# Masked queries in two halves, a product split around a score row, and row statistics one maximum later

## The chip, the cores and the metric

The kernel runs on one core of a Trainium2 chip. The metric is the device time of one execution in microseconds. A core has four compute engines that run their own in-order instruction streams and meet only at semaphores: TensorE (PE in the profile, its weight loads PEld), VectorE (DVE), ScalarE (ACT) and GpSimd (POOL). SyncE (SP) starts the transfers.

## The reference

32 sequences of 100 query rows and 361 context rows, width 256, pass through four layers. Each layer adds its result to x:

```python
x = x + xattn0(layernorm(x), ctx)       # 16 heads of 16, softmax(q k^T / 4) v
x = x + ffn0(layernorm(x))              # one of 8 experts per token, by argmax
x = x + xattn1(layernorm(x), ctx)       # 8 heads of 32, own layernorms and output product
x = x + ffn1(layernorm(x))              # two of 8 gated experts per token

# the part that the change touches, xattn0, for one sequence:
Q = layernorm(x) @ Wq + bq;  K, V = split(ctx @ Wkv + bkv)
scores = einsum('qhd,khd->hqk', Q, K) / 4      # 16 heads
out = einsum('hqk,khd->qhd', softmax(scores), V)
```

## The kernel before

The function `attention` is built twice, for layer 0 (the first attention) and layer 1. It takes one sequence, called a batch, at a time, and it is pipelined by hand: the step of batch b ("a round") does the front of batch b+1, the body of batch b, the tail of batch b-1, and prepares the context and rows of batch b+2. The names are `nxt` = b+1, `nxt2` = b+2, `prev` = b-1. Every engine has its own `step` (for VectorE `step0` in layer 0), and the order in which it calls things is the order of execution. Rounds run from t = -1 to 32. A tail is there from t = 1 on, and a batch t+2 to prepare until t = 29, so that both are there in the 29 rounds from 1 to 29. Rounds 4 to 27 are a loop on each engine, the others are written out.

What a round of layer 0 contains, as far as the change touches it:

- **Queries.** TensorE projects them into PSUM bank M0. ScalarE writes them with their bias to `qf` (L680), one instruction for each of the two 128-channel halves, and signals `qf_ready` after the second. VectorE multiplies `qf` by a mask, so that a group of 32 partitions holds one head of 16 at a time, into `QM` (L999, `masked_queries`), 128 partitions by 400 elements in one instruction.
- **Exact maxima.** Softmax needs each row's maximum. TensorE computes the scores of two heads at a time into the two banks of SM (`score_rows`, L453, rows 0 to 7), VectorE reduces them (`maxima`, L1008). SM holds only one pair, so row j waits for maximum j-1 (`max_done`), and maximum j waits for row j. Rows 0 and 1 read the first half of `QM`, row 2 the first of those that read the second.
- **Values.** The value product has three tiles of keys. `project_rest` (tile 2) and `project_first` (tile 0, into M0, so after `qf` has been read) are six matmuls each (L383), and both stand between row 0 and row 1 on TensorE. Then come `scores(b, 1)` (L478, L485), row 2, and so on.
- **Finished rows.** The rows of `prev` need their mean and variance: VectorE's `residual_stats(prev)` (L970, L977, L978) signals `var_ready`. GpSimd's `power(1, prev)` waits for it and runs four small instructions (L780, L786, L788, L792).
- **GpSimd's order.** `masked_max(b)`, `attended(prev)` (L808, adds the attention's output to the rows), `power(1, prev)`, `low_parts(nxt)` (L843, L848), `power(0, nxt2)`, `low_context(nxt2)` (L854, writes `cl`, the low part of the context), `attended_twice`, `masked_low`, `value_bias`. It is strictly in this order.
- **Keys of the batch after next.** After row 6, TensorE's `start_k` calls `first_k(nxt2)`, whose first instruction waits for `cl_ready`, which is what L854 signals. Behind it stand row 7, the transposes of `avs`, and the `front` of the next round.

```python
def first_k(b):
    pe.wait_ge(cl_ready, b.count(1, 1))
    project_k(b, 0)
```

Of the kernel before, what the change touches and what calls it, by code (L numbers as in the profile page):

```python
# [19 lines left out]
ALU = mybir.AluOpType  # L20
ACT = mybir.ActivationFunctionType
# [107 lines left out]
def attention(nc, layer, t, env):  # L129
# [7 lines left out]
    NG = H // HG  # L137
    NP = H // 2
    NS = 3
    AHEAD = 5 + layer  # L140
    SCALE = 0.25 if layer == 0 else 1.0 / 16.0
    LAG = 2 * layer
# [16 lines left out]
    with ExitStack() as ctx:  # L159
# [216 lines left out]

        @block.tensor
        def _(pe):
            def summed(out, pairs):

                steps = [(c, lhs, rhs) for c in range(DC) for lhs, rhs in pairs]
                for k, (c, lhs, rhs) in enumerate(steps):
                    last = nc.tensor.matmul(out, lhs(c), rhs(c), start=(k == 0), stop=(k == len(steps) - 1))  # L383
                return last

# [7 lines left out]

                summed(M1[:, 0:LKP], [(w(wkh), x(ch)), (w(wkh), x(cl)), (w(wkl), x(ch))]).then_inc(k_ps, 1)

            def project_v(b, kt, M, c0):
                k0, n = KTILES[kt]

                def x(context):
                    return lambda c: context[b.p][:, c, k0:k0 + n]  # L400

                def w(weights):
                    return lambda c: weights[:, c, :]

                return summed(M[0:n, c0:c0 + D], [(x(ch), w(wvh)), (x(ch), w(wvl)), (x(cl), w(wvh))])

            def first_k(b):
                pe.wait_ge(cl_ready, b.count(1, 1))
# [25 lines left out]
            def project_rest(b):  # L434
                project_v(b, 2, M1, D).then_inc(v_ps, 1)

            def project_first(b):
                pe.wait_ge(qf_ready, b.count(1, 1))
                last = project_v(b, 0, M0, 0)
                if layer == 1:  # L440
                    for c in range(DC):
                        last = nc.tensor.transpose(M0[0:LQ, D + c * 128:D + (c + 1) * 128], qf[:, c, :], ident[:])
                last.then_inc(v_ps, 1)

            def score_rows(b, j):

                if j == 0:
                    pe.wait_ge(kt_ready, b.count(1, 1))
                    pe.wait_ge(qm_ready, b.count(1, 1))
                pe.wait_ge(max_done, b.count(NP, j))  # L450
                for half in range(2):
                    rows, chunk, m = place(half * NP + j)
                    last = nc.tensor.matmul(SM[0:LQ, half, 0:LKP], QM[b.p][rows, chunk, m, :], KT[b.p][rows, chunk, :],  # L453
                                            start=True, stop=True)
                last.then_inc(sm_ps, 1)
# [88 lines left out]
            def step(b, fr, ahead, back, tail):  # L544
                nxt, nxt2, prev = b.plus(1), b.plus(2), b.plus(-1)

                def rows_of(*pairs):
                    if fr:
                        for j in pairs:
                            score_rows(nxt, j)  # L550

                if fr:
                    front(nxt)
                if back:
                    max_columns(b)
                if fr:
                    project(nxt)
                if back:
                    scores(b, 0)
                rows_of(*((0,), ())[layer])  # L560
                if fr:
                    project_rest(nxt)
                    project_first(nxt)
                rows_of(*((1,), (0,))[layer])
                if back:
                    scores(b, 1)
                rows_of(*((2,), (1,))[layer])
                if back:
                    free_m0(nxt, fr)
                    values(b, 0)  # L570
                rows_of(*((3,), ())[layer])
                if back:
                    scores(b, 2)
                rows_of(*((4,), (2,))[layer])
                if tail:
                    if fr:
                        pe.wait_ge(v_evac, nxt.count(2, 1))
                    out_transposes(prev, layer == 1, prev.low >= LAG)
                if back:
                    values(b, 1)  # L580
                rows_of(*((5,), ())[layer])
                if tail:
                    out_product(prev, layer == 1, prev.low >= LAG)
                if back:
                    values(b, 2).then_inc(av_ps, 1)
                rows_of(*((6,), (3,))[layer])
                if ahead:
                    start_k(nxt, nxt2, prev, tail)
                rows_of(*((7,), ())[layer])
                if back:  # L590
                    pe.wait_ge(avs_copied, b.count(1, 1))
                    for g in range(NG):
                        last = nc.tensor.transpose(ST[0:LQ, 0, g * 128:(g + 1) * 128], avs[:, g, :], ident[:])
                    last.then_inc(avt_ps, 1)
# [15 lines left out]
        def _(act):  # L610
# [7 lines left out]
            def split_k(b):  # L618

                act.wait_ge(k_evac, b.count(2, 2))  # L620
                if b.low >= 2:
                    act.wait_ge(st_ps, b.count(NS, -NS))
                nc.scalar.activation(KT[b.p][:], KF[:], ACT.Copy).then_inc(kt_ready, 1)  # L623
                act.wait_ge(qf_ready, b.count(1, 1))
                if layer == 0:
                    nc.scalar.activation(q_hi[:], qf[:], ACT.Copy).then_inc(q_hi_ready, 1)
                else:
                    nc.scalar.activation(QM[b.p][:, :, 0, :], qf[:], ACT.Copy).then_inc(qm_ready, 1)
# [45 lines left out]

            def projected(b):
                act.wait_ge(q_ps, b.count(1, 1))
                act.wait_ge(qm_ready, b.count(1))
                act.wait_ge(ql_ready, b.count(1))
                for h in range(DC):
                    last = nc.scalar.activation(qf[:, h, :], M0[:, h * LQ:(h + 1) * LQ], ACT.Identity,  # L680
                                                bias=bq[:, h:h + 1])
                last.then_inc(qf_ready, 1)
                split_k(b)

            def values_out(b):
# [83 lines left out]
        def _(pool):  # L769
# [68 lines left out]
            def low_parts(b):  # L838

                pool.wait_ge(kt_ready, b.count(1, 1))  # L840
                if b.low >= 2:
                    pool.wait_ge(st_ps, b.count(NS, -NS))
                nc.gpsimd.tensor_tensor(KL[b.p][:], KF[:], KT[b.p][:], ALU.subtract).then_inc(kl_ready, 1)  # L843
                if layer == 0:
                    pool.wait_ge(q_hi_ready, b.count(1, 1))
                    pool.wait_ge(qm_ready, b.count(1, 1))
                    pool.wait_ge(ql_ready, b.count(1))
                    nc.gpsimd.tensor_tensor(qf[:], qf[:], q_hi[:], ALU.subtract).then_inc(q_lo_ready, 1)  # L848

# [6 lines left out]
            def masked_low(b):  # L856

                if b.low >= 1:
                    pool.wait_ge(st_ps, b.count(NS))
                if layer == 1:  # L860
                    pool.wait_ge(qm_ready, b.count(1, 1))
                    nc.gpsimd.tensor_tensor(QL[:, :, 0, :], qf[:], QM[b.p][:, :, 0, :], ALU.subtract
                                            ).then_inc(ql_ready, 1)
                    return
                pool.wait_ge(q_lo_ready, b.count(1, 1))
                nc.gpsimd.tensor_tensor(
                    QL[:], qf[:].unsqueeze(2).to_broadcast([128, DC, HT, LQ]),
                    mask[:].unsqueeze(1).unsqueeze(3).to_broadcast([128, DC, HT, LQ]), ALU.mult).then_inc(ql_ready, 1)
# [86 lines left out]
        def _(dve):  # L955
# [37 lines left out]
                norm_stats(0, b, xrow(b))  # L993

            def masked_queries(b):
                dve.wait_ge(qf_ready, b.count(1, 1))
                if b.low >= 2:
                    dve.wait_ge(st_ps, b.count(NS, -NS))
                V_.tensor_tensor(  # L999
                    QM[b.p][:], qf[:].unsqueeze(2).to_broadcast([128, DC, HT, LQ]),  # L1000
                    mask[:].unsqueeze(1).unsqueeze(3).to_broadcast([128, DC, HT, LQ]), ALU.mult).then_inc(qm_ready, 1)

            def maxima(b, j):
                if j == 0:
# [84 lines left out]
            def step0(b, fr, ahead, back, tail):  # L1089
# [3 lines left out]
                for j in range(NP):  # L1093
                    if tail and j == 6:
                        take_product(prev, False, True)
                    if fr:
                        maxima(nxt, j)
                    if tail and j == 0:
                        residual(prev)
                        residual_stats(prev)  # L1100
                    if ahead and j == 1:
                        if nxt2.low == 1:
                            dve.wait_ge(x_more_loaded, 16)
                        moments(xrow(nxt2))
                    if ahead and j == 2:
                        variance(0, nxt2)
                if fr:
                    repeat_max(nxt)
# [1044 lines left out]
```

## Time and profile before

| | us |
|---|---|
| median of three runs | 1679.92 |
| lowest and highest | 1678.1, 1680.39 |
| the profiled execution | 1681.28 |
| its span, first to last instruction | 1679.5 |
| of it first attention | up to about 530 |
| second attention | about 820 to 1330 |

The profiled execution is 1.36 us above the median, and 1.78 us of its time lie outside its span. Busy time of an engine is a share of the whole span and says nothing of one stage. In a timeline the idle time in brackets is that of the engine just before the instruction, and the arrow names what it waited for; "issue" means that nothing in the profile shows a cause.

### The profile page before, as it was taken

Reading aid. Unit: us, or ns where it says so; the run is one execution under the profiler, and the core shown is the slowest. Engines: PE = TensorE matmul, PEld = TensorE weight load, DVE = VectorE, ACT = ScalarE, POOL = GpSimd, SP = SyncE. Lnnn points to the kernel's source line nnn. Section 1 sums busy time; section 2 is a strip of 40 time slices with the busy share of each in tenths; the row PEclk is TensorE's granted clock in tenths of the full one; section 3 lists DMA queues with packets and bytes.
Section 4 is the critical chain, followed back from the end, with each engine's and each line's share of the span. In section 5 each row is a group of like instructions: output and inputs, shape, how many; then the busy total and the mean of one; then the engine's idle time right before and its main releaser. Section 6 shows DMA issues by size and latency. Waiting matters only on the chain. (4 is left out here: it accounts for less than half of the span.)

```text
span 1679.5 us, 50228 instructions
## 1 busy us (share of the span) xinstructions
PE 1479.6 (88%) x17142; PEld 1237.9 (74%) x17143; DVE 985.4 (59%) x2196; ACT 880.9 (52%) x1626; POOL 838.1 (50%) x1145
## 2 busy tenths in 40 slices
PE   6999999999998299999689999999999925999958
PEld 4777777777776199999668888888888713888746
DVE  3666666666664323333236777777777558777745
ACT  3677777777775144444156566656665422333333
POOL 3566766656664111111146666666766414333275
PEclk7999999999998599999889999999999855999979
DMA  5121121111000611111212222222111041333377
GB/s 145 35 73 59 53 78 59 48 34 34 23 26 9 257 32 37 37 34 35 72 46 61 78 73 90 73 66 73 40 48 34 18 144 49 130 129 129 117 233 236
DMA packets 63184, 127.98 MB, mean 76 GB/s; under 512 B 11106, under 2 KB 35870, under 8 KB 59590
## 3 DMA queue, kind: packets, MB, share of 16 engines
q1 hardware_dynamic: 52798, 99.03, 18.1%
q0 software_dynamic: 10320, 28.07, 6.0%
q8 instruction: 41, 0.67, 0.2%
q14 instruction: 25, 0.20, 0.0%
HBM read 94.77 MB, written 32.29 MB: 76 GB/s over the span
## 5 line engine op out<-in xcount | busy, mean ns | idle before, releaser
L1008 DVE TENSOR_REDUCE a_mx<-a_SM 100x2 bf16<-100x722 f32 x384 | 351.4, 915 | 219.9 <-PE a_SM L453 215.2
L730 ACT ACTIVATE a_Pr<-a_ST 120x1600 f32<-120x1600 f32 (+3 forms) x192 | 225.0, 1172 | 134.6 <-PE a_ST L485 132.7
L780 POOL TENSOR_TENSOR a_rstd<-a_ve,a_powers 100x1 f32<-100x1 f32 x192 | 119.1, 620 | 161.5 <-DVE a_ve L978 161.3
L453 PE MATMUL a_SM<-a_KT,a_QM 32*100 32x362 f32 x768 | 155.4, 401 | 44.6 <-DVE a_mx L1008 40.0
L495 PE MATMUL a_M<-a_Pr,a_V 120*32 120x100 f32 (+3 forms) x4608 | 176.9, 257 | 0.0
L495 PEld LDWEIGHTS a_M<-a_Pr,a_V 120*32 120x32 f32 (+3 forms) x4608 | 136.3, 121 | 21.4 <-issue 12.7
L453 PEld LDWEIGHTS a_SM<-a_KT,a_QM 32*100 32x100 f32 x768 | 62.6, 159 | 102.2 <-DVE a_mx L1008 75.9
L854 POOL TENSOR_TENSOR a_cl<-a_ct,a_ch 128x724 fp32r<-128x724 f32 x62 | 107.2, 1728 | 43.1 <-DVE a_o L1050 43.1
L1531 PEld LDWEIGHTS e_PH<-e_xT,e_wS 128*128 128x128 f32 x1024 | 120.7, 194 | 4.4 <-issue 2.8
L1531 PE MATMUL e_PH<-e_xT,e_wS 128*128 128x128 f32 x1024 | 121.2, 277 | 2.3 <-DVE e_xT L1610 2.3
L383 PE MATMUL a_M<-a_wvh,a_ch 128*120 128x256 f32 (+1 forms) x384 | 120.9, 315 | 2.6 <-ACT a_KF L615 2.6
L1544 PE MATMUL e_PY<-w,e_hT 128*128 x512 | 117.7, 384 | 2.6 <-issue 2.6
L843 POOL TENSOR_TENSOR a_KL<-a_KF,a_KT 128x724 fp32r<-128x724 f32 x64 | 111.0, 1734 | 16.0 <-ACT a_KT L623 16.0
L383 PE MATMUL a_M<-a_ch,a_wkh 128*128 128x362 f32 x256 | 99.3, 388 | 18.3 <-POOL a_cl L935 18.1
L383 PE MATMUL a_M<-a_wvl,a_ch 128*120 128x256 f32 (+1 forms) x384 | 108.8, 283 | 0.0
L383 PE MATMUL a_M<-a_wvh,a_cl 128*120 128x256 f32 (+1 forms) x384 | 108.6, 283 | 0.0
L1544 PEld LDWEIGHTS e_PY<-w,e_hT 128*128 128x128 f32 x512 | 96.0, 192 | 15.3 <-issue 3.2
L485 PE MATMUL a_ST<-a_QM,a_KT 32*120 32x100 f32 (+3 forms) x1536 | 103.5, 305 | 0.0
L1575 ACT ACTIVATE e_hT<-e_PH,e_b 128x128 f32<-128x128 f32 x128 | 36.5, 368 | 124.4 <-PE e_PH L1531 124.4
L1497 POOL COPY e_gidx<-toks 128x1 int32 (+1 forms) x32 | 5.8, 181 | 189.8 <-PE e_PX L1518 166.2
L615 ACT ACTIVATE a_KF<-a_M,a_bk 128x362 f32<-128x362 f32 x128 | 71.7, 560 | 47.8 <-PE a_M L383 47.6
L1818 PE MATMUL g_PH<-w_high,g_xTh 128*128 x228 | 96.3, 422 | 0.0
(219 smaller groups left out, 3860.6 us busy)
## 6 DMA issues: line engine op xcount, KB each, us to landing
w<-in_E_w SPq DMA_DIRECT2D x24, 1024.0 KB, 6.9
a_ct<-in_ctx SPq DMA_DIRECT2D x64, 362.0 KB, 3.0
gated_rows<-g_hs SPq DMA_DIRECT2D x57, 256.0 KB, 2.4
keep_rows<-a_keep SPq DMA_DIRECT2D x64, 100.0 KB
tile_rows<-e_y SPq DMA_DIRECT2D x32, 128.0 KB
X<-in_E_b SPq DMA_DIRECT2D x1, 4096.0 KB, 17.6
x_rows<-X SPq DMA_DIRECT2D x32, 100.0 KB
g_xr<-x_rows SPq DMA_DIRECT2D x25, 128.0 KB, 3.8
```

The lines of the kernel that those rows point to most:

```text
L383: last = nc.tensor.matmul(out, lhs(c), rhs(c), start=(k == 0), stop=(k == len(steps) - 1))
L453: last = nc.tensor.matmul(SM[0:LQ, half, 0:LKP], QM[b.p][rows, chunk, m, :], KT[b.p][rows, chunk, :], start=True, stop=True)
L485: last = nc.tensor.matmul(ST[0:n, r, t * LQ:(t + HT) * LQ], K[rows, chunk, k0:k0 + n], Q[rows, chunk, :, :], start=False, stop=(k == 2 and ...
L495: last = nc.tensor.matmul(M0[VW * j:VW * (j + 1), g * LQ:(g + 1) * LQ], V[b.p][0:n, kt, h, :], Pr[0:n, kt, POS[h] * LQ:(POS[h] + 1) * LQ], ...
L730: nc.scalar.activation(Pr[0:n, s, :].rearrange("p (r q) -> p r q", r=GROUPS), ST[0:n, :, 0:PER * LQ], ACT.Exp, scale=SCALE).then_inc(exp_d ...
L780: nc.gpsimd.tensor_tensor(rstd[k][:], ve[k][:].to_broadcast([LQ, n]), powers[:, 0:n], ALU.pow).then_inc(rstd_ready[k], 1)
L843: nc.gpsimd.tensor_tensor(KL[b.p][:], KF[:], KT[b.p][:], ALU.subtract).then_inc(kl_ready, 1)
L854: nc.gpsimd.tensor_tensor(cl[b.p][:], ct[b.p][:], ch[b.p][:], ALU.subtract).then_inc(cl_ready, 1)
L1008: V_.tensor_reduce(pair, SM[0:LQ, :, 0:LK], AX_X, ALU.max).then_inc(max_done, 1)
L1531: last = nc.tensor.matmul(PH[:, p, g // 4, g % 4, :], lhs, xT[:, c, :], start=(c == 0), stop=(c == DC - 1))
L1544: last = nc.tensor.matmul(PY[:, p, 0:D], hT[p][:, g, :], rhs, start=(g == 0), stop=(g == G - 1))
L1818: last = nc.tensor.matmul(PH[:, p, h, :], x[p][:, c, :], rhs, start=(k == 0), stop=(k == len(steps) - 1))
```

## The change

The masked queries are made in two instructions, one for each half of the channels, and each can start when ScalarE has written its half of `qf`. Row 0 waits for the first half only, and row 2 has a wait of its own for the second. The value product of the first tile of keys is cut in two: three matmuls before row 1 and three behind it. The statistics of the finished rows move from behind maximum 0 to behind maximum 1, and those of the batch after next by one maximum as well (moments behind maximum 2, variance behind maximum 3). In layer 1 only the count of `qf_ready` changes. All of the diff but its context lines, with the places where only a count changed cut to one each:

```diff
+    QS = 2 - layer
...
-            def summed(out, pairs):
+            def summed(out, pairs, part=None):
                 steps = [(c, lhs, rhs) for c in range(DC) for lhs, rhs in pairs]
                 for k, (c, lhs, rhs) in enumerate(steps):
+                    if part is not None and c != part:
+                        continue
...
-            def project_first(b):
-                pe.wait_ge(qf_ready, b.count(1, 1))
-                last = project_v(b, 0, M0, 0)
+            def project_first(b, part=None):
+                pe.wait_ge(qf_ready, b.count(DC, DC))
+                last = project_v(b, 0, M0, 0, part)
...
-                last.then_inc(v_ps, 1)
+                if part != 0:
+                    last.then_inc(v_ps, 1)
             def score_rows(b, j):
                 if j == 0:
                     pe.wait_ge(kt_ready, b.count(1, 1))
-                    pe.wait_ge(qm_ready, b.count(1, 1))
+                    pe.wait_ge(qm_ready, b.count(QS, 1))
+                if layer == 0 and j == HT:
+                    pe.wait_ge(qm_ready, b.count(QS, 2))
...
                 if fr:
                     project_rest(nxt)
-                    project_first(nxt)
+                    project_first(nxt, (0, None)[layer])
                 rows_of(*((1,), (0,))[layer])
+                if fr and layer == 0:
+                    project_first(nxt, 1)
                 if back:
                     scores(b, 1)
...
                 for h in range(DC):
-                    last = nc.scalar.activation(qf[:, h, :], M0[:, h * LQ:(h + 1) * LQ], ACT.Identity,
-                                                bias=bq[:, h:h + 1])
-                last.then_inc(qf_ready, 1)
+                    nc.scalar.activation(qf[:, h, :], M0[:, h * LQ:(h + 1) * LQ], ACT.Identity,
+                                         bias=bq[:, h:h + 1]).then_inc(qf_ready, 1)
...
             def masked_queries(b):
-                dve.wait_ge(qf_ready, b.count(1, 1))
                 if b.low >= 2:
                     dve.wait_ge(st_ps, b.count(NS, -NS))
-                V_.tensor_tensor(
-                    QM[b.p][:], qf[:].unsqueeze(2).to_broadcast([128, DC, HT, LQ]),
-                    mask[:].unsqueeze(1).unsqueeze(3).to_broadcast([128, DC, HT, LQ]), ALU.mult).then_inc(qm_ready, 1)
+                for h in range(DC):
+                    dve.wait_ge(qf_ready, b.count(DC, h + 1))
+                    V_.tensor_tensor(
+                        QM[b.p][:, h], qf[:, h, :].unsqueeze(1).to_broadcast([128, HT, LQ]),
+                        mask[:].unsqueeze(2).to_broadcast([128, HT, LQ]), ALU.mult).then_inc(qm_ready, 1)
...
-                    if tail and j == 0:
+                    if tail and j == 1:
                         residual(prev)
                         residual_stats(prev)
-                    if ahead and j == 1:
+                    if ahead and j == 2:
                         if nxt2.low == 1:
                             dve.wait_ge(x_more_loaded, 16)
                         moments(xrow(nxt2))
-                    if ahead and j == 2:
+                    if ahead and j == 3:
                         variance(0, nxt2)
```

## Rows read from the trace of the kernel before

**Rows 1.** The profile's page, part 1, busy time by engine.

```profile
PE 1479.6 (88%) x17142; PEld 1237.9 (74%) x17143; DVE 985.4 (59%) x2196; ACT 880.9 (52%) x1626; POOL 838.1 (50%) x1145
```

**Rows 2.** Windows: stretch, length, then busy us (instructions) by engine, clock, DMA, GB/s.

```profile
32.00:48.00 16.00, 12.61 (x191) 10.34 (x194) 6.04 (x10) 8.94 (x14) 5.97 (x7) 0.70 0.04 11
48.00:64.00 16.00, 15.06 (x260) 12.19 (x257) 10.64 (x20) 11.42 (x20) 8.55 (x13) 1.00 0.08 27
66.50:512.00 445.50, 420.03 (x6946) 339.87 (x6944) 290.51 (x560) 319.60 (x561) 292.34 (x393) 1.00 0.16 48
```

**Rows 3.** Waits of 0 to 560 us: us in total, times, longest us.

```profile
POOL a_rstd L780 <- DVE a_ve L978: 85.6, 34, 5.8
PE a_SM L453 <- DVE a_QM L999: 3.9, 12, 0.4
```

**Rows 4.** Timeline, VectorE, 214.8 to 218.3: start, duration, instruction [idle before it <- releaser].

```profile
214.85 0.92 DVE L1008 TENSOR_REDUCE a_mx<-a_SM 100x2 bf16<-100x722 f32 x1 [0.74 <-PE a_SM L453]
...
216.49 0.15 DVE L978 TENSOR_SCALAR a_ve<-a_mv 100x1 f32<-100x1 f32 x1
216.80 0.92 DVE L1008 TENSOR_REDUCE a_mx<-a_SM 100x2 bf16<-100x722 f32 x1 [0.16 <-PE a_SM L453]
...
218.22 0.92 DVE L1008 TENSOR_REDUCE a_mx<-a_SM 100x2 bf16<-100x722 f32 x1 [0.17 <-PE a_SM L453]
```

**Rows 5.** Timeline, GpSimd, 216.7 to 223.7 us.

```profile
216.73 0.71 POOL L780 TENSOR_TENSOR a_rstd<-a_ve,a_powers 100x2 f32<-100x2 f32 x1 [3.04 <-DVE a_ve L978]
...
217.99 0.26 POOL L788 TENSOR_SCALAR a_nmr<-a_mv,a_rstd 100x1 f32<-100x1 f32 x1
...
220.98 0.55 POOL L780 TENSOR_TENSOR a_rstd<-a_ve,a_powers 100x1 f32<-100x1 f32 x1
...
221.96 1.73 POOL L854 TENSOR_TENSOR a_cl<-a_ct,a_ch 128x724 fp32r<-128x724 f32 x1
```

**Rows 6.** Timeline, TensorE and its weight loads, 215.7 to 225.3 us.

```profile
215.79 0.28 PE L383 MATMUL a_M<-a_wvh,a_cl 128*121 128x256 f32 x1
...
216.15 0.28 PE L383 MATMUL a_M<-a_wvh,a_cl 128*121 128x256 f32 x1
...
216.35 0.41 PE L453 MATMUL a_SM<-a_KT,a_QM 32*100 32x362 f32 x2
...
217.78 0.40 PE L453 MATMUL a_SM<-a_KT,a_QM 32*100 32x362 f32 x2 [0.23 <-DVE a_mx L1008]
...
224.04 0.19 PEld L383 LDWEIGHTS a_M<-a_ch,a_wkh 128*128 128x128 f32 x1 [0.17 <-issue]
...
225.23 0.16 PEld L453 LDWEIGHTS a_SM<-a_KT,a_QM 32*100 32x100 f32 x2 [0.23 <-DVE a_mx L1008]
```

**Rows 7.** Timeline, the first round with finished rows, and the last of the 29.

```profile
63.26 1.73 POOL L854 TENSOR_TENSOR a_cl<-a_ct,a_ch 128x724 fp32r<-128x724 f32 x1
...
65.11 0.19 PEld L383 LDWEIGHTS a_M<-a_ch,a_wkh 128*128 128x128 f32 x1 [0.37 <-issue]
...
510.58 0.19 PEld L383 LDWEIGHTS a_M<-a_ch,a_wkh 128*128 128x128 f32 x1 [0.17 <-issue]
```

**Rows 8.** Timeline, two rounds that follow each other, around the masked queries.

```profile
212.95 0.73 POOL L808 TENSOR_TENSOR X<-X,a_o 100x256 f32 x1
213.03 1.08 DVE L999 TENSOR_TENSOR a_QM<-a_qf,a_mask 128x400 fp32r<-128x400 f32 x1 [1.59 <-ACT a_qf L680]
...
214.41 0.41 PE L453 MATMUL a_SM<-a_KT,a_QM 32*100 32x362 f32 x2 [0.35 <-DVE a_QM L999]
...
229.19 0.58 DVE L999 TENSOR_TENSOR a_QM<-a_qf,a_mask 128x400 fp32r<-128x400 f32 x1 [1.57 <-ACT a_qf L680]
...
230.59 0.92 DVE L1008 TENSOR_REDUCE a_mx<-a_SM 100x2 bf16<-100x722 f32 x1 [0.82 <-PE a_SM L453]
```

**Rows 9.** Timeline, ScalarE, 219.0 to 220.5 us.

```profile
219.01 0.59 ACT L646 ACTIVATE a_xp<-X,a_nmr,a_rstd 100x256 f32 x1
220.45 1.51 ACT L730 ACTIVATE a_Pr<-a_ST 120x1600 f32<-120x1600 f32 x1 [0.85 <-PE a_ST L485]
```

More of the change, by code:

```diff
@@ L394, in project_k, with project_v @@
                 summed(M1[:, 0:LKP], [(w(wkh), x(ch)), (w(wkh), x(cl)), (w(wkl), x(ch))]).then_inc(k_ps, 1)
-            def project_v(b, kt, M, c0):
+            def project_v(b, kt, M, c0, part=None):
                 k0, n = KTILES[kt]
@@ L403, in w @@
                     return lambda c: weights[:, c, :]
-                return summed(M[0:n, c0:c0 + D], [(x(ch), w(wvh)), (x(ch), w(wvl)), (x(cl), w(wvh))])
+                return summed(M[0:n, c0:c0 + D], [(x(ch), w(wvh)), (x(ch), w(wvl)), (x(cl), w(wvh))], part)
             def first_k(b):
@@ L623, in split_k @@
                 nc.scalar.activation(KT[b.p][:], KF[:], ACT.Copy).then_inc(kt_ready, 1)
-                act.wait_ge(qf_ready, b.count(1, 1))
+                act.wait_ge(qf_ready, b.count(DC, DC))
                 if layer == 0:
@@ L676, in projected @@
                 act.wait_ge(q_ps, b.count(1, 1))
-                act.wait_ge(qm_ready, b.count(1))
+                act.wait_ge(qm_ready, b.count(QS))
                 act.wait_ge(ql_ready, b.count(1))
                 for h in range(DC):
-                    last = nc.scalar.activation(qf[:, h, :], M0[:, h * LQ:(h + 1) * LQ], ACT.Identity,
-                                                bias=bq[:, h:h + 1])
-                last.then_inc(qf_ready, 1)
+                    nc.scalar.activation(qf[:, h, :], M0[:, h * LQ:(h + 1) * LQ], ACT.Identity,
+                                         bias=bq[:, h:h + 1]).then_inc(qf_ready, 1)
                 split_k(b)
@@ L845, in low_parts @@
                     pool.wait_ge(q_hi_ready, b.count(1, 1))
-                    pool.wait_ge(qm_ready, b.count(1, 1))
+                    pool.wait_ge(qm_ready, b.count(QS, QS))
                     pool.wait_ge(ql_ready, b.count(1))
@@ L860, in masked_low @@
                 if layer == 1:
-                    pool.wait_ge(qm_ready, b.count(1, 1))
+                    pool.wait_ge(qm_ready, b.count(QS, QS))
                     nc.gpsimd.tensor_tensor(QL[:, :, 0, :], qf[:], QM[b.p][:, :, 0, :], ALU.subtract
```

## The prediction

> **What bounds the kernel now.** I read the page's busy times first: TensorE works 88% of the span, every other engine under 60% [rows 1]. The windows say how full it is where the change is made: 420.0 of 445.5 us, 94%, at the full clock (2.4 GHz), in the stretch that holds 28 rounds [rows 2]. So there is about 0.9 us of TensorE idle time per round to win, and the change only reorders; it takes no matmul away. The waits come next. GpSimd is idle for 85.6 us in front of its first power instruction, waiting for VectorE's variance of the finished rows [rows 3], the very thing that the change makes later. The timeline of one round then shows what each late start would touch. I count from maximum 0 of a round, here 214.85 [rows 4].
>
> - The variance (L978) starts at 216.49, 1.64 after maximum 0; GpSimd's power starts 0.24 later, having been idle for 3.04 us [rows 4, 5].
> - From there GpSimd has no slack: the four small instructions, L843, L848, the next power, its product and L854 follow each other, and `cl` is finished at 221.96 + 1.73 = 223.69 [rows 5]. That is 7.20 us behind the variance's start and 8.84 behind maximum 0.
> - TensorE loads the first weights of `first_k`, which waits for `cl`, at 224.04 [rows 6], 0.35 behind its end. What a real wait leaves between them is seen in round 1, where GpSimd was a little later: `cl` ended at 63.26 + 1.73 = 64.99 and the load came at 65.11, 0.12 later [rows 7]. So the usable slack of this chain is 0.35 - 0.12 = 0.23 us. It is this number that decides.
>
> The 3.04 us for which GpSimd is idle look like room, but they lie ahead of the chain, and the chain's start is what moves.
>
> **The change part by part.**
>
> *Statistics one maximum on.* They cost the same, but begin behind maximum 1 instead of behind maximum 0. The split product lets row 1 start sooner: it starts at 216.35 now, 0.20 behind the start of the twelfth matmul of the two products (216.15), though maximum 0 ended at 214.85 + 0.92 = 215.77. The ninth started at 215.79 [rows 4, 6]. With three matmuls moved behind it, row 1 can start 0.20 behind the ninth, at 215.99, and maximum 1 is 0.36 sooner than now, 1.95 - 0.36 = 1.59 behind maximum 0. The bounds are 1.42, the distance of maxima whose row waits only for its maximum (216.80 and 218.22) [rows 4, 6], and 1.95, no move at all. I take 1.59. So the variance starts 1.59 later, at 3.23 behind maximum 0. `cl` is ready at 3.23 + 7.20 = 10.43, and `first_k` starts at 10.55, against 9.19 now: TensorE stands still for about 1.35 us in front of it. Queued behind `first_k` are row 7, hence maximum 7, the repeated maxima, the avs transposes and the whole front of the next round. None of it can slip ahead.
>
> *What happens from `first_k` to the next maximum 0.* In the round that ends at 230.59 this took 230.59 - 224.04 = 6.55 us, with no wait for the masked queries; the other kind of round waits 0.35 us for them in front of row 0, and there are 12 such waits, 3.9 us in all [rows 3, 6, 8]. Row 7's weight load, which now has 0.23 us of waiting for maximum 6 in front of it [rows 6], finds that maximum long done. TensorE itself had no gap there, so I take 0.05 of it. 6.50 for every round. New period: 10.55 + 6.50 = 17.05 us.
>
> *Masked queries in halves.* The instruction takes 0.58 us when it starts ahead of GpSimd's L808, and 1.08 when L808 has started 0.08 before it [rows 8]. The first half can start when the first half of `qf` is there, earlier by one ScalarE instruction, so ahead of L808 in either round, and it does not have to wait. By the rows this is worth 0.4 us in every other round. The bounds are nothing (the half still collides) and 3.9 us over the stage, plus what the odd rounds are longer by. VectorE issues one instruction more; the nearest row gives it between 0.29 (half of 0.58) and 0.58 us, into idle time of 1.6 us in front and 0.7 behind [rows 4, 8]. I take no cost for it.
>
> The Trainium skill (SBUF — State Buffer, "SBUF: two separate sides") says that VectorE and GpSimd share a pair of ports by an exclusive lock, and the one that starts first holds it for its whole instruction. The two durations above agree. By that rule the first half escapes the wait and the second may be caught behind L808, up to 0.7 us, which row 2, three microseconds on, doesn't notice. Without it half of the rounds would keep their 0.4 us: 14 x 0.4 = 5.6 us more in the sum.
>
> *The split product.* The same six matmuls. What row 1 gains on its way (0.36 us) is spent before `first_k` and lost in the wait there. Only rounds outside the 29 keep it: the two at the start and round 30. 3 x 0.36 = 1.1 us of gain. The extra waits (for `qf` behind row 1, for the second half at row 2) are satisfied when reached. The nearest row of a satisfied wait shows 0.17 us on the weight queue alone [rows 6]; two of them lie before the stall. Nothing to 0.3 us, taken as nothing.
>
> *The other engines.* ScalarE's L646 for the finished rows needs GpSimd's product and lies at 219.01 now, behind the second exponential [rows 9]. That product was ready at 217.99 + 0.26 = 218.25 [rows 5]; 1.59 later is 219.84, and L646 takes 0.59, to about 220.5. The third exponential starts at 220.45 [rows 9], so it is pushed by less than 0.1. If it were pushed by 0.5, the values that follow it on TensorE would still be done before `first_k` may start, since all of that lies ahead of the stall; so it costs nothing, and the same holds for the input rows on ScalarE. VectorE's second statistics come one maximum later too, ahead of GpSimd's late second power (220.98 + 1.59 = 222.57) [rows 5]. No step that moved issues a transfer. SyncE's load of a context behind `cl_ready` is issued 1.35 us later and is used two rounds on.
>
> *Sum.* Round 1 is late by the full 1.59, since it already waited [rows 7]. The 28 periods between its `first_k` and that of round 29 took 510.58 - 65.11 = 445.47 us [rows 7], 15.91 each (the loop's two kinds of round, and shorter ones outside it). They become 28 x 17.05 = 477.4. Change: 477.4 - 445.5 + 1.6 - 1.1 = +32.4 us. On the profiled execution, 1681.28 with its span of 1679.5, that is 1713.7; it was 1.36 above the median, so 1712.3 for the median. The second attention only counts a semaphore differently and costs nothing.
>
> **The rivals.**
>
> 1. *The cover holds, and it is faster.* It needs the chain from variance to `cl` to have 1.59 us of slack. Then 12 rounds lose their 0.4 us wait (4.5 us) and all 29 about 0.2 us, the wait of row 2 for maximum 1 [rows 6]: -10, 1670. For it: GpSimd's 3.04 us of idle time. Against it: 0.35 between `cl` and its reader. It turns to slower as soon as the chain is late by more than about 0.23 + 0.4 us.
> 2. *The stall is paid and given back.* If the waits behind `first_k` (0.74 us of VectorE before maximum 0 [rows 4], 0.35 of TensorE) were not behind it in order but beside it, half of the stall would be absorbed: 29 x 0.6 = +17, 1697. Against it: everything there descends from `first_k` or stands behind it in a queue.
> 3. *Row 1 does not move up.* If it still starts 1.5 us behind maximum 0, the statistics are late by 1.95 instead of 1.59: 29 x 0.36 more, +10, 1723. Against it: row 1 follows the last product at 0.20 [rows 6], so fewer products must bring it forward.
> 4. *The clock falls.* TensorE would be busy 15.0 of 17.05 us, 88%. It ran at full clock at 94% (15.06 of 16) and partly at half (1.2 GHz) in the window with 79%, where it completed 191 matmuls against 260 [rows 2]. At that pace a round takes 17.05 x 260 / 191 = 23.2: 29 x 6.2 = 180 more, about 1892. The Trainium skill (TensorE: Matmul & The Clock Gate, "What's actually happening") makes the half rate the default and activity what lifts it. By that rule the stall would have to count as inactivity.
> 5. *Nothing measurable.* The chain is late by just what the faster rows give back. 1680.
>
> **How the numbers follow.** The forecast has 82%, the rivals in their order 4, 5, 4, 2 and 3%. The forecast's own bounds: down by 0.17 us per round if row 1 waits only for maximum 0 (1.42) and by 0.1 if row 7's whole wait is saved, 28 x 0.27 = 7.6, to 1704.7; up by 5.6 if the halves still collide, to 1717.9. With a microsecond of scatter I give 1703.5 to 1719. A change under 0.2% (3.4 us) is about what this kernel's measurement cannot tell from none. Faster 4%, same 3%, slower 93%.
>
> **What would show it.** In the profile after: the lines of waits have TensorE or its weight queue idle for about 1.3 us in front of L383 for GpSimd's `cl`, 29 times. Maximum 1 starts 1.59 behind maximum 0, the variance 3.23, `cl` ends at 10.43, and rounds are 17.05 us long without two kinds. The first masked half is not stretched. Layer 1 and the expert stages keep their times. I am wrong if `first_k` is not released by GpSimd, if the row after the split waits for something else, or if ScalarE's late L646 holds the third exponential back by more than some tenths (that would come on top).

## The result

The changed kernel takes 1725.84 us (median of four runs, 1721.02 to 1729.78) against 1680.03 for the kernel before: a ratio of 1.027, 95% interval 1.0255 to 1.0287. It is slower by 45.8 us; forecast were 32.4 us and a range that ends at 1719. The profiled execution took 1729.78, with a span of 1728.0.

The page after, part 1, answers to [rows 1]: the same number of matmuls, with TensorE busy 23 us longer, since part of them ran slower.

```profile
PE 1502.2 (87%) x17142; PEld 1248.7 (72%) x17143; DVE 1000.5 (58%) x2228; ACT 883.4 (51%) x1626; POOL 835.7 (48%) x1145
```

The waits of 0 to 610 us after the change answer to [rows 3]. TensorE's wait for `cl` is new, 29 times; GpSimd's wait for the variance is longer; no row waits for the masked queries any more.

```profile
POOL a_rstd L787 <- DVE a_ve L985: 133.9, 34, 8.4
...
PE a_M L386 <- POOL a_cl L861: 37.7, 29, 1.8
```

The timeline after the change: the first weight load of `first_k` in round 1, a round that nothing disturbs, whose maximum 0 is at 165.00, and `first_k` in round 29. The lines of `attention` lie a little lower now: L808 is L815, L843 is L850, L854 is L861, L978 is L985, L999 is L1007, L1008 is L1016.

```profile
67.84 0.19 PEld L386 LDWEIGHTS a_M<-a_ch,a_wkh 128*128 128x128 f32 x1 [1.99 <-issue]
...
165.00 0.92 DVE L1016 TENSOR_REDUCE a_mx<-a_SM 100x2 bf16<-100x722 f32 x1 [0.22 <-PE a_SM L459]
...
166.59 0.92 DVE L1016 TENSOR_REDUCE a_mx<-a_SM 100x2 bf16<-100x722 f32 x1 [0.67 <-PE a_SM L459]
...
168.23 0.15 DVE L985 TENSOR_SCALAR a_ve<-a_mv 100x1 f32<-100x1 f32 x1
...
168.46 0.71 POOL L787 TENSOR_TENSOR a_rstd<-a_ve,a_powers 100x2 f32<-100x2 f32 x1 [3.91 <-DVE a_ve L985]
...
173.71 1.71 POOL L861 TENSOR_TENSOR a_cl<-a_ct,a_ch 128x724 fp32r<-128x724 f32 x1
...
175.48 0.43 PE L386 MATMUL a_M<-a_ch,a_wkh 128*128 128x362 f32 x1 [1.26 <-POOL a_cl L861]
175.75 0.33 PE L386 MATMUL a_M<-a_cl,a_wkh 128*128 128x362 f32 x1
175.92 0.32 PE L386 MATMUL a_M<-a_ch,a_wkl 128*128 128x362 f32 x1
...
561.36 0.19 PEld L386 LDWEIGHTS a_M<-a_ch,a_wkh 128*128 128x128 f32 x1 [1.64 <-issue]
```

Maximum 1 starts 1.59 behind maximum 0, the variance 3.23, `cl` ends at 173.71 + 1.71 = 175.42, which is 10.42, and `first_k` starts at 10.48, after TensorE has stood for 1.26 us. Forecast were 1.59, 3.23, 10.43 and 10.55 (before: [rows 4 to 6]). The windows below (columns as in [rows 2]) hold one round each: that one, one two rounds later and the one right behind it. The last holds the 28 rounds.

```profile
165.00:182.00 17.00, 15.16 (x249) 11.99 (x249) 10.95 (x21) 11.44 (x21) 10.31 (x14) 1.00 0.11 28
199.00:218.60 19.60, 17.97 (x249) 14.42 (x249) 10.65 (x22) 11.43 (x21) 10.40 (x14) 0.83 0.10 27
218.60:237.00 18.40, 16.72 (x249) 13.24 (x250) 10.89 (x22) 11.53 (x21) 10.30 (x14) 0.91 0.23 82
...
67.80:561.40 493.60, 444.59 (x6945) 352.41 (x6945) 304.16 (x588) 321.63 (x560) 289.07 (x393) 0.96 0.14 44
```

The same 249 matmuls, the same work on every other engine, but a round takes 19.6 or 18.4 us instead of 17.0, and the granted clock (the mean share of its full rate that TensorE was given) is 0.83 or 0.91 instead of 1.00. The half rate (1.2 GHz) shows in the single matmuls of TensorE there:

```profile
209.40 0.67 PE L386 MATMUL a_M<-a_ch,a_wkh 128*128 128x362 f32 x1 [1.26 <-POOL a_cl L861]
209.87 0.50 PE L386 MATMUL a_M<-a_cl,a_wkh 128*128 128x362 f32 x1
210.17 0.51 PE L386 MATMUL a_M<-a_ch,a_wkl 128*128 128x362 f32 x1
```

These matmuls of 362 columns start 0.47 and 0.30 us apart, and the second and third take about 0.50; the same three of the undisturbed round (175.48, 175.75 and 175.92 above) start 0.27 and 0.17 apart, and take about 0.33. Windows drawn around the stall show that the clock fell in it: it is 1.00 up to 209.05 and 0.50 from 209.07 on, and TensorE stands still until 209.40. It is back at 1.00 from 215.9 on, and falls a second time at 229.5, 0.5 us behind the end of the next round's stall (0.50 up to 232.9). Between rounds 1 and 29 there are such stretches in four places: in the first rounds up to 110 us, and near 209, 349 and 489 us, each over about two rounds.

### The profile page after: what moved, and what is told of

Read it like the earlier page. It is cut to its first block and busy times, and to the rows that moved or that the text cites. A ratio compares the mean times of both kernels' runs of the same rounds, so it can differ in the third digit from the quotient of the medians.

```text
span 1728.0 us, 50328 instructions
## 1 busy us (share of the span) xinstructions
PE 1502.2 (87%) x17142; PEld 1248.7 (72%) x17143; DVE 1000.5 (58%) x2228; ACT 883.4 (51%) x1626; POOL 835.7 (48%) x1145
## 5 line engine op out<-in xcount | busy, mean ns | idle before, releaser
L1016 DVE TENSOR_REDUCE a_mx<-a_SM 100x2 bf16<-100x722 f32 x384 | 351.4, 915 | 251.9 <-PE a_SM L459 248.8
L386 PE MATMUL a_M<-a_ch,a_wkh 128*128 128x362 f32 x256 | 104.7, 409 | 55.3 <-POOL a_cl L861 37.7
L861 POOL TENSOR_TENSOR a_cl<-a_ct,a_ch 128x724 fp32r<-128x724 f32 x62 | 106.6, 1719 | 42.9 <-DVE a_o L1058 42.9
L850 POOL TENSOR_TENSOR a_KL<-a_KF,a_KT 128x724 fp32r<-128x724 f32 x64 | 111.4, 1740 | 15.4 <-ACT a_KT L631 15.4
L654 ACT ACTIVATE a_xh<-X,a_nmr,a_rstd 100x256 f32 (+1 forms) x64 | 38.4, 601 | 132.3 <-POOL a_nmr L795 132.2
L386 PEld LDWEIGHTS a_M<-a_ch,a_wkh 128*128 128x128 f32 x256 | 53.8, 210 | 68.4 <-POOL a_cl L861 36.2
```

What stands on the lines that cost most here:

```text
L861: nc.gpsimd.tensor_tensor(cl[b.p][:], ct[b.p][:], ch[b.p][:], ALU.subtract).then_inc(cl_ready, 1)
L1016: V_.tensor_reduce(pair, SM[0:LQ, :, 0:LK], AX_X, ALU.max).then_inc(max_done, 1)
```

## The experiments

Eleven kernels ran. Their times stand beside runs of the kernel before on the same chip (its medians were 1679.7 to 1681.6). "Round" is the mean of the 28 periods from `first_k` of round 1 to that of round 29 in the profile, "clock" is the granted clock of that stretch.

| kernel | us | ratio to before | round | clock |
|---|---|---|---|---|
| before | 1680.0 | 1 | 15.91 | 1.00 |
| changed | 1725.8 | 1.027 | 17.63 | 0.96 |
| late statistics alone | 1775.7 | 1.054 | 19.21 | 0.90 |
| halves alone | 1671.6 | 0.995 | 15.67 | 1.00 |
| split product alone | 1671.7 | 0.995 | 15.55 | 1.00 |
| halves and split, statistics back | 1668.8 | 0.993 | 15.55 | 1.00 |
| changed, finished rows' statistics back | 1668.9 | 0.994 | 15.56 | 1.00 |
| changed, L850 before the powers | 1694.0 | 1.008 | 16.29 | 1.00 |
| the same, ordered behind the halves | 1672.2 | 0.994 | 15.64 | 1.00 |
| statistics back, `cl` late otherwise | 1721.5 | 1.024 | 17.31 | 0.98 |
| changed, 16 matmuls in the stall | 1711.5 | 1.018 | 16.98 | 1.00 |
| changed, 6 matmuls in the stall | 1713.3 | 1.019 | 17.07 | 0.99 |
| late statistics alone, 20 matmuls | 1727.3 | 1.028 | 17.56 | 1.00 |

### The parts alone

**Late statistics alone.** On the kernel before:

```diff
-                    if tail and j == 0:
+                    if tail and j == 1:
                         residual(prev)
...
-                    if ahead and j == 1:
+                    if ahead and j == 2:
...
-                    if ahead and j == 2:
+                    if ahead and j == 3:
                         variance(0, nxt2)
```

> The kernel before with the statistics one maximum on and nothing else. Theory A (the late variance makes cl late, TensorE stands before first_k, and the stalls now and then halve its clock): without the split product maximum 1 is 1.95 behind maximum 0, so the variance starts at 3.59 and cl ends at 10.8; rounds are 17.3 to 17.8 us, +42 to +53, and the clock adds 10 to 40: 1730 to 1775. Theory B (the two halves or the split product carry a good part of the 45.8 us): below 1715.

1775.66 (1757.97 to 1781.55), interval of the ratio 1.0495 to 1.0588, 0.7 us above the end of theory A's range. One edit of the three is worth more than the whole loss. The windows show how: undisturbed rounds of 17.4 and 17.8 us, others of 18.9 to 20.4 us at a clock of 0.83 to 0.91. The stall in front of `first_k` is 1.26 us, as in the changed kernel, and not 1.65: the other 0.4 us are waits of TensorE for maxima before it, since maximum 2 starts 3.69 behind maximum 0 and not 3.33.

```profile
191.00:209.00 18.00, 15.43 (x255) 12.23 (x249) 10.61 (x20) 11.93 (x21) 10.23 (x15) 1.00 0.24 85
...
247.00:267.50 20.50, 18.14 (x249) 14.74 (x250) 10.39 (x21) 11.62 (x21) 10.18 (x14) 0.83 0.07 23
...
72.00:606.50 534.50, 467.45 (x6920) 378.75 (x6919) 286.40 (x555) 317.75 (x556) 287.05 (x391) 0.90 0.13 40
```

**Halves alone.** The kernel before with the new `masked_queries` and its waits:

```diff
-                V_.tensor_tensor(QM[b.p][:], ...)
+                for h in range(DC):
+                    dve.wait_ge(qf_ready, b.count(DC, h + 1))
+                    V_.tensor_tensor(QM[b.p][:, h], ...)
```

> The kernel before with the masked queries in two halves and nothing else. Theory A: the first half escapes GpSimd's L808, the 12 waits of row 0 go, 1674 to 1677. Theory B: the pair of halves is longer than the one instruction and holds row 2 or maximum 0 back, 1683 or more.

1671.63 (1670.36 to 1672.41), ratio 0.9934 to 0.996. Faster, and 2.4 us under theory A's range: the rounds are 15.58 and 15.75 us long, where the kernel before has 15.75 and 16.15.

**Split product alone.**

```diff
                     project_rest(nxt)
-                    project_first(nxt)
+                    project_first(nxt, (0, None)[layer])
                 rows_of(*((1,), (0,))[layer])
+                if fr and layer == 0:
+                    project_first(nxt, 1)
```

> The kernel before with the product split around row 1 and nothing else; the statistics stay behind maximum 0. Theory A: row 1 is early but maximum 1 must wait for the statistics on VectorE, so it starts 1.80 instead of 1.95 behind maximum 0, and this is hidden from there on: 1677 to 1681. Theory B: the waits and the second group cost TensorE some tenths per round, 1684 or more.

1671.7 (1666.57 to 1674.35), ratio 0.9933 to 0.9964. That is 5 us better than either theory. Maximum 1 was at 1.74, close to the forecast, and `first_k` 0.11 earlier, but the larger part is that the masked queries no longer collide, although nothing was done to them:

```profile
192.37 0.58 DVE L1004 TENSOR_TENSOR a_QM<-a_qf,a_mask 128x400 fp32r<-128x400 f32 x1 [1.48 <-ACT a_qf L686]
...
208.00 0.58 DVE L1004 TENSOR_TENSOR a_QM<-a_qf,a_mask 128x400 fp32r<-128x400 f32 x1 [1.48 <-ACT a_qf L686]
```

They take 0.58 us in every round. The collision with GpSimd's L808 in every other round before [rows 8] was a race of a tenth of a microsecond, and any edit that shifts the two may end it.

**Halves and split, all statistics back.** On the changed kernel:

```diff
-                    if tail and j == 1:
+                    if tail and j == 0:
                         residual(prev)
...
-                    if ahead and j == 2:
+                    if ahead and j == 1:
...
-                    if ahead and j == 3:
+                    if ahead and j == 2:
                         variance(0, nxt2)
```

> The changed kernel with all statistics back where they were; halves and split stay. Theory A: no wait for cl is left, the clock stays full in the stage, the gains of the halves remain: 1672 to 1678. Theory B: most of the 45.8 us stays, 1700 or more.

1668.78 (1666.73 to 1671.97), ratio 0.9915 to 0.9941. Below theory A's range; with the next kernel the fastest of all, and faster than both kernels of this case. The chain to `cl` is still close:

```profile
204.46 1.73 POOL L861 TENSOR_TENSOR a_cl<-a_ct,a_ch 128x724 fp32r<-128x724 f32 x1
...
206.42 0.19 PEld L386 LDWEIGHTS a_M<-a_ch,a_wkh 128*128 128x128 f32 x1 [0.17 <-POOL a_cl L861]
```

`cl` ends at 206.19 and is used at 206.42. Of the 0.23 us between them 0.1 are usable if the bare delay is 0.12 [rows 7], and 0.18 if it is the 0.05 of the loop's rounds after the change (175.42 and 175.48 above). A later start of that chain would not be free here either.

**Only the finished rows' statistics back.** On the changed kernel:

```diff
-                    if tail and j == 1:
+                    if tail and j == 0:
                         residual(prev)
```

> The changed kernel with the finished rows' statistics alone back behind maximum 0; the moments and variance of the batch after next stay one maximum later. If only the start of GpSimd's chain matters: the same as with all statistics back, 1667 to 1672, since the second power is reached 6.1 us behind maximum 0 and its variance is there at 5.7. If the second statistics delay the chain as well: rounds longer by some tenths, 1676 or more.

1668.88 (1665.49 to 1672.39). The same as with all statistics back, so this one line carries the whole loss, and the statistics of the batch after next can be late for nothing.

### Is it the late `cl`?

**Another cause for a late `cl`.** Statistics back, but GpSimd does L854's subtraction twice:

```diff
             def low_context(b):
...
+                if layer == 0 and b.low >= 2:
+                    nc.gpsimd.tensor_tensor(spare[:], ct[b.p][:], ch[b.p][:], ALU.subtract)
                 nc.gpsimd.tensor_tensor(cl[b.p][:], ct[b.p][:], ch[b.p][:], ALU.subtract).then_inc(cl_ready, 1)
```

> The kernel with halves and split product but statistics where they were (1669), with L854's subtraction done twice, once into a spare tile, so that cl is late by 1.7 us for a reason that has nothing to do with statistics. Theory A: first_k waits; rounds of 8.86 + 1.7 + 0.06 + 6.47 = 17.1 us instead of 15.55, +43, and stalls of 1.5 us that let the clock fall in some rounds: 1712 plus 10 to 50, 1720 to 1765. Rival (it is the late statistics, not the late cl): below 1685.

1721.48 (1717.24 to 1723.79), inside theory A's range and far above the rival's. With `cl` ending 10.50 to 10.53 behind maximum 0 the undisturbed rounds are 16.95 to 17.16 us, and in its profile two places have longer ones, 18.46 and 18.61, 19.70 and 18.47. These four cost about 7 us over undisturbed ones, less than the 10 to 50 that I expected of the clock. The stall is longer than in the changed kernel (1.4 against 1.26 us) and the falls are fewer, so its length alone does not set their number.

```profile
168.15 1.74 POOL L864 TENSOR_TENSOR a_spare<-a_ct,a_ch 128x724 fp32r<-128x724 f32 x1
169.83 1.73 POOL L865 TENSOR_TENSOR a_cl<-a_ct,a_ch 128x724 fp32r<-128x724 f32 x1
171.61 0.43 PE L388 MATMUL a_M<-a_ch,a_wkh 128*128 128x362 f32 x1 [1.43 <-POOL a_cl L865]
```

**Late statistics with the cover restored.** GpSimd does `low_parts` before the powers, in the time in which it waits for the variance:

```diff
+                if fr and layer == 0:
+                    low_parts(nxt)
                 if tail and layer == 0:
                     power(1, prev)
...
-                if fr:
+                if fr and layer == 1:
                     low_parts(nxt)
```

> The changed kernel, statistics still late, but GpSimd does low_parts (L843 and L848, 2.3 us) ahead of the power instructions that wait for the late variance, where it is idle. Theory A (the order on GpSimd turns a late variance into a late cl): cl ends at 3.23 + 7.20 - 2.3 = 8.1 behind maximum 0, before TensorE asks for it; no wait for cl, no fall of the clock, 1668 to 1675. Rival (the late statistics cost by themselves, on VectorE or ScalarE): 1690 or more.

1694.0 (1692.83 to 1695.73). The number lies in the rival's range, but what the trace shows is neither theory. The wait for `cl` is gone: `cl` is ready 0.4 us before `first_k` loads. The rounds of the loop are now 15.5 and 16.9 us long by turns, and there is another loss in the long ones. A round of 15.5 us first, then one of 16.9:

```profile
187.35 1.35 DVE L1009 TENSOR_TENSOR a_QM<-a_qf,a_mask 128x200 fp32r<-128x200 f32 x2 [1.25 <-ACT a_qf L688]
...
188.44 1.89 POOL L850 TENSOR_TENSOR a_KL<-a_KF,a_KT 128x724 fp32r<-128x724 f32 x1
...
202.91 3.13 DVE L1009 TENSOR_TENSOR a_QM<-a_qf,a_mask 128x200 fp32r<-128x200 f32 x2 [1.24 <-ACT a_qf L688]
203.26 0.86 POOL L815 TENSOR_TENSOR X<-X,a_o 100x256 f32 x1
...
204.08 1.74 POOL L850 TENSOR_TENSOR a_KL<-a_KF,a_KT 128x724 fp32r<-128x724 f32 x1
...
205.97 0.90 DVE L1018 TENSOR_REDUCE a_mx<-a_SM 100x2 bf16<-100x722 f32 x1
```

In the long rounds the two masked halves take 3.13 us. The second half lasts through L815 and then through L850, which follows at once, and maximum 0, in order behind it on VectorE, starts at 205.97, though its row was there at 204.6. In the short rounds the pair takes 1.35 us, and it is L850 that is longer, 1.89 us instead of 1.74. The Trainium skill (SBUF — State Buffer, "SBUF: two separate sides") says that the one that starts first has the shared ports for its whole instruction. That fits both kinds of round, one waiting for the other; the trace adds that a waiting VectorE does not always get its turn between two GpSimd instructions. What decides it stays open: L850 starts 0.83 us behind L815 in the short round and 0.82 in the long one.

**The same, with a wait** in `low_parts` in front of L850, so that both halves are done first:

```diff
+                if layer == 0:
+                    pool.wait_ge(qm_ready, b.count(QS, QS))
```

> As the run with low_parts ahead of the powers (1694), but GpSimd waits for both masked halves before L843, so that VectorE's second half can't be caught behind two GpSimd instructions (the pair took 3.1 us there). Theory A': that run had no wait for cl any more and lost its time only in this collision: the pair is back at 1.3 us, max 0 is not late, first_k starts at 9.1 behind it, 1667 to 1674, although the statistics are as late as in the changed kernel. Rival (late statistics have a price of their own): 1685 or more.

1672.19 (1670.28 to 1675.07), ratio 0.9923 to 0.9956. The statistics are as late as in the changed kernel (3.25 behind maximum 0) and there is no loss against the kernel before. `first_k` asks for `cl` 0.41 us after it is there. That settles the first part: late statistics cost by way of GpSimd's order. If they cost anything beside it, it is hidden in the 3.4 us between this kernel and the one with all statistics back (1668.8), which were timed on different chips.

```profile
188.81 1.74 POOL L863 TENSOR_TENSOR a_cl<-a_ct,a_ch 128x724 fp32r<-128x724 f32 x1
...
190.96 0.19 PEld L386 LDWEIGHTS a_M<-a_ch,a_wkh 128*128 128x128 f32 x1 [0.17 <-issue]
...
195.78 1.43 DVE L1011 TENSOR_TENSOR a_QM<-a_qf,a_mask 128x200 fp32r<-128x200 f32 x2 [1.24 <-ACT a_qf L688]
```

### What is the rest?

**The stall filled.** The changed kernel with unused matmuls between row 6 and the wait for `cl` (their result is overwritten later):

```diff
             def start_k(nxt, nxt2, prev, tail):
...
+                    if layer == 0:
+                        for k in range(16):
+                            nc.tensor.matmul(ST[:, 3, 0:128], ones_bf[:], ones_bf[:], start=True, stop=True)
```

> The changed kernel with 16 extra matmuls (bf16, 128x128 by 128 columns, result unused) on TensorE between row 6 and the wait for cl, in the place where it stands still for 1.3 us; they should take about 1 us and end before cl is there. Theory A: the stall itself is 16.95 - 15.91 us per round and stays, but TensorE is no longer idle in it, so the clock stays full: all rounds 16.95, 1708 to 1713, and the runs scatter less. Rival (the clock falls for another reason, or the excess over the predicted 32 us has another cause): as the changed kernel, 1721 to 1730, or longer by what the matmuls take.

1711.45 (1708.83 to 1714.02), ratio 1.0166 to 1.02, as theory A has it. More work on TensorE, and 14 us less time. `cl` is as late as before, and 0.29 us of idle time are left:

```profile
184.71 1.72 POOL L864 TENSOR_TENSOR a_cl<-a_ct,a_ch 128x724 fp32r<-128x724 f32 x1
185.13 1.07 PE L548 MATMUL a_ST<-a_ones_bf 128*128 128x128 bf16 x16
...
186.49 0.43 PE L386 MATMUL a_M<-a_ch,a_wkh 128*128 128x362 f32 x1 [0.29 <-POOL a_cl L864]
```

The window over the 28 rounds has the clock at 1.00, where the changed kernel had 0.96:

```profile
67.60:543.00 475.40, 453.33 (x7393) 361.46 (x7393) 305.21 (x588) 321.39 (x560) 289.77 (x393) 1.00 0.15 45
```

**Six matmuls** instead of 16 in the same place.

> The changed kernel with 6 extra matmuls instead of 16, which take 0.4 us and leave about 0.9 us of the stall. If the clock falls whenever the idle time of a round passes some size between 0.3 and 1.3 us, this run lies either with the filled one (1711) or with the changed one (1726); a value between, 1713 to 1722, means fewer falls of the same kind. My guess is 1711 to 1717.

1713.34 (1712.79 to 1715.04). The longest waits for `cl` are 1.2 us and the sum 24.5, but its profile has one long round (19.82) in place of the nine of the changed kernel between 18.38 and 19.88. 1713.34 is inside my guess. An idle time of 0.84 us (24.5 / 29) instead of 1.3 kept nearly all of the clock.

**The late statistics alone, with 20 matmuls.**

> The kernel before with the late statistics alone (1775.7), with 20 extra matmuls in the place of the stall (1.3 of its 1.65 us). If the rest over the stall is the clock: rounds of 10.85 + 6.55 to 6.95 = 17.4 to 17.8 throughout, 28 x 17.6 = 493 against 445.5, 1725 to 1733. If the clock is not kept up by it: above 1755.

1727.27 (1726.26 to 1731.23), in the range of the first case, and 48 us less than the same kernel without them (1.028 against 1.054, each over its own runs of the kernel before).

```profile
72.00:580.00 508.00, 468.24 (x7741) 380.48 (x7744) 298.48 (x578) 327.01 (x572) 301.20 (x405) 1.00 0.14 42
```

## Why the prediction was wrong

- **What bounds, and the slack of 0.23 us:** right. The stall in front of `first_k` is there in each of the 29 rounds, 37.7 us in all, and disappears when either the statistics go back or `cl` no longer depends on them.
- **Statistics one maximum on:** right, term by term: 1.59, 3.23 and 10.42 against 10.43. Only what lies between the end of `cl` and `first_k` was 0.05 in the loop's rounds, not the 0.12 that I read in a round written out.
- **From `first_k` to maximum 0:** 6.39 and 6.55 by turns, mean 6.47, for 6.50. Undisturbed rounds are 16.87 and 17.02, mean 16.95 for 17.05. There are still two kinds, against what I wrote, but without the wait for the queries.
- **The sum without the clock:** 28 x 16.95 = 474.6 against 445.5. The filled kernel, where the clock stays at full rate, measures it: 1711.45, or +31.8 us over its runs of the kernel before. Forecast were +32.4. That these agree to 0.6 us is in part luck. In the filled kernel's profile the 28 rounds add 475.35 - 445.47 = 29.9 us, where I had 31.9, and the start adds 2.5 (its first `first_k` of round 1 is at 67.62, before at 65.11), where I had 1.6 - 1.1.
- **The step that failed** is rival 4, the clock. I gave it 2%, and all or nothing: half the rate for the whole stage, +180 us. So the sum held nothing for the clock, and neither did the range. It came in part. In the profiled execution, the slowest of the four, the 28 rounds took 561.36 - 67.84 = 493.5 us, 18.9 more than 28 undisturbed ones, nearly all of it in the nine rounds of 18.38 to 19.88 us. Over the runs it is 1725.84 - 1711.45 = 14.4 us. The windows from which I argued had 79% and 94% of busy time [rows 2], and 88% lay between them. From those rows I should have priced a partial fall, which reaches from nothing to +180, and set the upper end of the range by it. The price of the full fall was loose as well: the window with 79% has a clock of 0.70 [rows 2], so it ran at the half rate for only 60% of its time. The Trainium skill (TensorE: Matmul & The Clock Gate, "What's actually happening") has activity lift the clock; the filled kernels agree, since with the added matmuls the clock is 1.00 where it was 0.96 and 0.90.
- **Masked queries in halves, split product:** both gain, 9 us each alone and 12 together, which is less than the sum. In the changed kernel they make row 1 earlier, and so the variance (3.23 instead of 3.59), one reason why it loses 46 us and not 95. My rival 1, in which the cover holds, was priced at 1670; the kernels without a wait for `cl` that keep both (all statistics back; `low_parts` early and ordered) have 1669 and 1672. In the changed kernel's profile the pair of halves takes about 1.4 us, and no row waits for it. The third exponential starts 5.70 behind maximum 0 and not 5.60, so the late L646 cost ScalarE 0.1, as forecast.
- **The start:** round 1's `first_k` came 2.7 us later than before, for my 1.6 and some gain. One execution tells little of it: in the two kernels with the finished rows' statistics back, which differ only in the second statistics, it is at 66.3 and 61.3 us, with a clock of 0.81 and 0.93 between 14 and 60 us. What lies behind round 29 took 1166.6 us in the profile and 1168.9 before.

What stays open is which rounds the fall hits. The places near 209, 349 and 489 us are 140 us apart; nothing here tells why those, nor why a longer stall in the kernel with the doubled subtraction had fewer falls. The execution times of the changed kernel scatter by 9 us, those of the kernel before by 5.

## What to carry to other kernels

Idle time in front of an engine that waits is not slack if what stands behind the wait is a chain without gaps whose last product is asked for at once: measure the distance between the last instruction's end and its reader, and let that decide about moving the first. When a small stall is added to every round of a kernel that keeps TensorE busy, price the clock too, as a fall in some of the rounds. And before moving an operation on GpSimd forward, see what VectorE has pending against it there.

## What the runs showed of the hardware

- In the kernel whose TensorE stood still for 1.3 us in every round of 17, its clock fell to half (1.2 GHz) in some of them (0.96 over the stage). With the late statistics alone, where the stall is the same but an undisturbed round is longer (17.4 to 17.8 us), it did so in more (0.90). With the doubled subtraction, where the stall is 1.4 us, it did so in fewer (0.98). The first two, filled up with unused matmuls, kept 1.00, and took 14 and 48 us less.
- A VectorE instruction with two SBUF inputs that found GpSimd busy waited through two GpSimd instructions in a row in every other round of the loop (the pair of halves took 3.13 us), and in the rounds between through the first alone (1.35 us).
- When VectorE's masked queries and GpSimd's L808 started within a tenth of a microsecond of each other, their order decided 0.5 us of VectorE's time and 0.4 us of every other round [rows 8]; with the split product alone, which touches neither, they took 0.58 us in every round.
